# Six elementwise operations of the back stages issued on GpSimd instead of VectorE, with the beats planned anew

## The reference

```python
x = x + layernorm(attn(layernorm(x)))     # a selective state space layer ("front" and "back")
x = x + layernorm(ffn(layernorm(x)))      # mixture of low-rank experts ("back" and "last")

def attn(x, ...):                          # di = 512, N = 16 states
    h = x * rsqrt(mean(x * x) + EPS) * norm_scale
    xs, res = split(h @ w_in, 2)
    res, xs = silu(res), silu(causal_depthwise_conv(xs) + b)
    delta, B, C = split(xs @ w_xproj, ...)
    delta = softplus(delta @ w_dt + b_dt)
    ys = scan over the 512 tokens of (exp(delta * A), delta * xs * B), per channel and state
    out = (sum over the states of ys * C + xs * D) * res
    return x + out @ w_out

def ffn(x, ...):                           # two branches of 8 experts of rank 64
    prod = (x @ V_k) * cumsum(x @ W_k over tokens)
    weights = softmax(gelu(x @ r1 + b1) @ r2 + b2 + expert_bias)
    out = sum over k of (prod * weights) @ U_k + weights @ b
    return out / n_valid                   # n_valid = 1 .. number of the token
```

## Time and profile before

| | us |
|---|---|
| median of 3 runs | 2735.68 |
| lowest and highest run | 2731.32, 2737.05 |
| the profiled execution: first to last instruction | 2733.1 |
| VectorE busy in it | 2470.7 (90%) |
| TensorE busy (matmuls) | 2233.0 (82%) |
| ScalarE busy | 1718.4 (63%) |
| GpSimd busy | 1638.1 (60%) |

### The profile page before, as it was taken

How to read it: one execution, slowest core, us unless ns; L and a number is a source line. 1 busy time by engine, 2 the same in 40 slices (tenths; PEclk the granted TensorE clock), 3 DMA queues, 4 the chain that set the end, 5 groups by cost and what they waited for, 6 DMA issues and landing times.

```text
span 2733.1 us, 35478 instructions
## 1 busy us (share of the span) xinstructions
PE 2233.0 (82%) x9268; PEld 1316.2 (48%) x9268; DVE 2470.7 (90%) x3315; ACT 1718.4 (63%) x3353; POOL 1638.1 (60%) x1083
## 2 busy tenths in 40 slices
PE   5666788888888888888888888888888888888798
PEld 2434355454544545454454545445454554545454
DVE  1699999999999999999999999999999999999951
ACT  3554675858567584766758476675847667584544
POOL 0667575757657575665757566575756757575610
PEclk9766899999999999999899998999999999999998
DMA  5011100101001010110101010010101001010100
GB/s 123 24 43 31 42 25 28 51 28 51 29 20 55 28 52 24 51 32 21 56 26 53 24 51 29 24 55 24 55 25 51 28 24 55 24 47 28 35 1 16
DMA packets 83410, 101.81 MB, mean 37 GB/s; under 512 B 23481, under 2 KB 49873, under 8 KB 83169
## 3 DMA queue, kind: packets, MB, share of 16 engines
q1 hardware_dynamic: 83168, 99.06, 12.2%
HBM read 90.13 MB, written 8.91 MB: 36 GB/s over the span
## 4 chain that ended last, share of the span: by engine, by line
DVE 37%; issue 27%; PE 14%; POOL 11%; ACT 5%; DVEq 1%; POOLq 0%; ACTq 0%
DVE h L1252 13%; DVE yT L1268 11%; PE bank L709 9%; POOL bx L680 7%; PE stateT L878 3%; DVE xs L1127 3%; DVE prod L1227 2%; ACT decay L1084 2%; ACT cum_sb L1049 2%; DVE res L1148 1%; DVE yT L1265 1%; POOL x_back L646 1%; DVE xs L1142 1%; PE bank L853 1%; DVE st L1107 1%
## 5 line engine op out<-in xcount | busy, mean ns | idle before, releaser
L680 POOL TENSOR_TENSOR bx<-dx,B_rows 128x1024 f32<-128x1024 f32 x512 | 1219.5, 2389 | 495.6 <-DVE h L1252 468.7
L1252 DVE TENSOR_TENSOR_SCAN h<-decay,bx 128x512 f32<-128x512 f32 x1024 | 1238.3, 1209 | 75.8 <-ACT decay L1084 52.0
L1084 ACT ACTIVATE decay<-delta,decay_rate 128x512 f32<-128x512 f32 x1024 | 706.8, 693 | 656.6 <-DVE h L1252 631.6
L878 PE MATMUL stateT<-ident,h 128*128 128x128 f32 x4096 | 683.6, 298 | 322.0 <-DVE h L1252 175.8
L878 PEld LDWEIGHTS stateT<-ident,h 128*128 128x128 f32 x4096 | 499.0, 150 | 725.5 <-issue 353.4
L1268 DVE SCALAR_TENSOR_TENSOR yT<-stateT,C_tok,yT 128x512 f32<-128x512 f32 x960 | 696.0, 725 | 16.3 <-PE stateT L878 16.0
L709 PE MATMUL bank<-q_to_expert,xnT 128*128 128x512 f32 x512 | 267.3, 649 | 12.5 <-ACT dx L988 12.4
L709 PE MATMUL bank<-k_to_expert,cumT 128*128 128x512 f32 x512 | 266.7, 647 | 9.3 <-DVE prod L1227 9.2
L709 PE MATMUL bank<-hT,w_in_sb 128*128 128x512 f32 x512 | 245.7, 610 | 18.1 <-DVE xs L1127 17.2
L1049 ACT ACTIVATE cum_sb<-bank,gate 128x64 f32<-128x64 f32 x1024 | 222.8, 329 | 39.4 <-PE bank L709 28.3
L853 PE MATMUL bank<-expert_to_out,prodT 128*128 128x256 f32 x1024 | 242.1, 379 | 0.4 <-ACT prodT L1059 0.4
(11 more groups left out here) (161 smaller groups left out, 2493.1 us busy)
## 6 DMA issues: line engine op xcount, KB each, us to landing
B_rows<-B_scratch SPq DMA_DIRECT2D x256, 256.0 KB, 3.2
x_front<-in_L_attn_x SPq DMA_DIRECT2D x16, 512.0 KB, 4.5
x_back<-in_L_attn_x SPq DMA_DIRECT2D x16, 512.0 KB, 5.1
out<-x_back SPq DMA_DIRECT2D x16, 512.0 KB, 3.3
w_in_sb<-in_L_attn_w_in SPq DMA_DIRECT2D x1, 1024.0 KB, 5.7
h<-in_L_ffn_V_fwd SPq DMA_DIRECT2D x2, 256.0 KB
h<-in_L_ffn_W_inv_exp SPq DMA_DIRECT2D x2, 256.0 KB
h<-in_L_ffn_W_fwd SPq DMA_DIRECT2D x2, 256.0 KB
```

The source lines that it names most:

```text
L680: pool.tensor_tensor(bx[use % BX_RING][:, :, :], dx[q.parity][:, 2 * half:2 * half + 2, :], row, ALU.mult).then_inc(s_bx.step(f"{n},{half} ...
L878: last = pe.transpose(stateT[j % 2][:, c * P:(c + 1) * P], h[n % 2][:, c, j * P:(j + 1) * P], ident[:, :])
L1084: act.activation(decay[c % 2][:, :], delta[q.parity][:, c, :], ACT.Exp, scale=decay_rate[:, c, n:n + 1]).then_inc(s_exp.step(f"{n},{c}"), 1)
L1252: dve.tensor_tensor_scan(h[n % 2][:, c, :], decay[c % 2][:, :], bx[(2 * n + c // 2) % BX_RING][:, c % 2, :], 0.0, ALU.mult, ALU.add).then_ ...
```

## The change

The six operations keep, o, x1, sub, sn and wa go from VectorE's list to GpSimd's, with their semaphore steps (b_dve to b_pool), and everyone who waits for them waits for the other semaphore. keep becomes a tensor_scalar multiplication by 1. n_valid is replaced by its reciprocal once in VectorE's prologue, so that rc takes the reciprocal of sm's result at once and sn multiplies after it; before, sn came first. In TIMETABLE many beats are new.

```diff
-    ("B", "keep", "dve"): (255,),
+    ("B", "keep", "pool"): (264,),
-    ("F", "rs", "pool"): (15,),
+    ("F", "rs", "pool"): (18,),
-    ("F", "x", "sp"): (86,),
+    ("F", "x", "sp"): (79,),
...
-    ("F", "dt", "act"): (89, 93, 107, 111),
-    ("F", "ex", "act"): (91, 94, 107, 119),
-    ("F", "ln", "act"): (92, 96, 107, 119),
+    ("F", "dt", "act"): (89, 90, 107, 114),
+    ("F", "ex", "act"): (91, 95, 107, 119),
+    ("F", "ln", "act"): (92, 96, 109, 119),
...
-    ("F", "row", "sp"): (102, 123, 126),
+    ("F", "row", "sp"): (99, 123, 126),
-    ("B", "u", "dve"): (263, 264, 264, 268),
-    ("B", "o", "dve"): (268, 270, 271, 271),
-    ("B", "wo", "pe"): (274, 278, 282, 287),
-    ("B", "r", "dve"): (283, 283, 287, 289),
-    ("B", "st", "dve"): (293,),
+    ("B", "u", "dve"): (263, 264, 264, 270),
+    ("B", "o", "pool"): (273, 275, 278, 278),
+    ("B", "wo", "pe"): (274, 280, 282, 287),
+    ("B", "r", "dve"): (283, 286, 287, 289),
+    ("B", "st", "dve"): (290,),
...
-    ("B", "t", "act"): (302,),
-    ("B", "x1", "dve"): (301,),
+    ("B", "t", "act"): (301,),
+    ("B", "x1", "pool"): (304,),
...
-    ("B", "rb1", "pool"): (309,),
-    ("B", "xn", "act"): (310,),
+    ("B", "rb1", "pool"): (317,),
+    ("B", "xn", "act"): (315,),
...
-    ("B", "gelu", "act"): (338,),
+    ("B", "gelu", "act"): (337,),
...
-    ("B", "lb", "dve"): (346,),
-    ("B", "mx", "dve"): (347,),
-    ("B", "sub", "dve"): (347,),
-    ("B", "ex", "act"): (348,),
-    ("B", "sm", "dve"): (349,),
-    ("B", "sn", "dve"): (351,),
-    ("B", "rc", "dve"): (352,),
-    ("B", "wa", "dve"): (353,),
+    ("B", "lb", "dve"): (345,),
+    ("B", "mx", "dve"): (346,),
+    ("B", "sub", "pool"): (354,),
+    ("B", "ex", "act"): (347,),
+    ("B", "sm", "dve"): (347,),
+    ("B", "sn", "pool"): (359,),
+    ("B", "rc", "dve"): (349,),
+    ("B", "wa", "pool"): (359,),
...
-    ("L", "t", "act"): (468,),
+    ("L", "t", "act"): (469,),
-    ("F", "dx", "pool"): (105, 113, 126, 127),
+    ("F", "dx", "pool"): (103, 111, 126, 127),
...
+            def keep_task(b, k, use):
+                if b.shift(-1).exists:
+                    pool.wait_ge(b_dve.sem, b_dve.done(b.shift(-1), "r3"))
+                pool.wait_ge(f_pool.sem, f_pool.done(b, "r1"))
+                pool.sem_inc(passed["pool"], 1)
+                pool.tensor_scalar(r_keep[:, :], r_x0[b.parity][:, :], 1.0, None, ALU.mult).then_inc(b_pool.step("keep"), 1)
+
+            def o_task(b, c, use):
+                r = b.parity
+                pool.wait_ge(b_dve.sem, b_dve.done(b, f"u{c}"))
+                pool.tensor_tensor(res[r][:, c, :], xs[r][:, c, :], res[r][:, c, :], ALU.mult).then_inc(b_pool.step(f"o{c}"), 1)
...
+            def sub_task(b, k, use):
+                pool.wait_ge(b_dve.sem, b_dve.done(b, "mx"))
...
             def wo_task(b, k, use):
                 if k == 0:
-                    pe.wait_ge(b_dve.sem, b_dve.done(b, "o3"))
+                    pe.wait_ge(b_pool.sem, b_pool.done(b, "o3"))
...
             def soft_exp(b, k, use):
-                act.wait_ge(b_dve.sem, b_dve.done(b, "sub"))
+                act.wait_ge(b_pool.sem, b_pool.done(b, "sub"))
...
                 dve.wait_ge(w_pool, 7)
+                dve.reciprocal(n_valid[:, :, :], n_valid[:, :, :]).then_inc(w_dve, 1)
```

More of the change, by code:

```diff
@@ L320, in program @@
         b_act = Steps(sem("b_act"), steps_of("act", "B", {"t": numbered("t"), "xn": numbered("xn"), "xnT": ["xnT{}"], "rt": ["rt{}"], "gelu": ["gelu"], "logit": ["lc"], "ex": ["ex"], "gT": ["gT"]}))
[L321 to L325, removed]
+        b_dve = Steps(sem("b_dve"), steps_of("dve", "B", {"u": ["u{}"], "r": ["r{}"], "st": numbered("st"),
+                                                          "ag": numbered("ag"), "st1": numbered("s1"), "ag1": numbered("a1"),
+                                                          "cum": ["cum{}"], "lb": ["lb"], "mx": ["mx"], "sm": ["sm"], "rc": ["rc"]}))
+        b_pool = Steps(sem("b_pool"), steps_of("pool", "B", {"keep": ["keep"], "o": ["o{}"], "rb": ["ve", "rb", "ng", "nm"], "x1": ["x1"],
+                                                             "rb1": ["ve1", "rb1", "ng1", "nm1"], "sub": ["sub"], "sn": ["sn"], "wa": ["wa"]}))
         l_pe = Steps(sem("l_pe"), steps_of("pe", "L", {"cum": ["cum{}"], "xv": ["xv{}"], "pt": ["pt{}"], "out": ["out{}"]}))
@@ L646, in x_task, with x1_task, sn_task, wa_task @@
                 pool.tensor_tensor(x_back[b.parity][:, half, :], x_back[b.parity][:, half, :], o_rows[:, half, :], ALU.add).then_inc(l_pool.step(f"x{k}"), 1)
+            def keep_task(b, k, use):
[8 more added lines that the diff above has]
+                pool.tensor_tensor(res[r][:, c, :], xs[r][:, c, :], res[r][:, c, :], ALU.mult).then_inc(b_pool.step(f"o{c}"), 1)
+            def x1_task(b, k, use):
+                pool.wait_ge(b_act.sem, b_act.done(b, "t3"))
+                pool.tensor_tensor(x_back[b.parity][:, :, :], x_back[b.parity][:, :, :], rows[:, :, :], ALU.add).then_inc(b_pool.step("x1"), 1)
+            flat_l = logits[:, :, :, :].rearrange("p a b k -> p (a b) k")
+            def sub_task(b, k, use):
+                pool.wait_ge(b_dve.sem, b_dve.done(b, "mx"))
+                pool.tensor_tensor(flat_l, flat_l, top[:, :].rearrange("p (a o) -> p a o", o=1).broadcast_to([P, TB * 2, KE]),
+                                   ALU.subtract).then_inc(b_pool.step("sub"), 1)
+            def sn_task(b, k, use):
+                pool.wait_ge(b_dve.sem, b_dve.done(b, "rc"))
+                pool.tensor_tensor(total[:, :], total[:, :], n_valid[:, :, :].rearrange("p a b -> p (a b)"), ALU.mult).then_inc(b_pool.step("sn"), 1)
+            def wa_task(b, k, use):
+                pool.wait_ge(b_pool.sem, b_pool.done(b, "sn"))
+                if b.shift(-1).exists:
+                    pool.wait_ge(l_act.sem, l_act.done(b.shift(-1), "cum7"))
+                pool.tensor_tensor(gate[:, :, :].rearrange("p a (b k) -> p (a b) k", k=KE), flat_l,
+                                   total[:, :].rearrange("p (a o) -> p a o", o=1).broadcast_to([P, TB * 2, KE]), ALU.mult).then_inc(b_pool.step("wa"), 1)
             def back_rstd(b, k, use):
@@ L810, in gateT_task @@
             def gateT_task(b, k, use):
-                pe.wait_ge(b_dve.sem, b_dve.done(b, "wa"))
+                pe.wait_ge(b_pool.sem, b_pool.done(b, "wa"))
                 if use.sem is b_dve.sem:
@@ L941, in xs_task @@
                     if b.shift(-2).exists:
-                        act.wait_ge(b_dve.sem, b_dve.done(b.shift(-2), "o3"))
+                        act.wait_ge(b_pool.sem, b_pool.done(b.shift(-2), "o3"))
                 act.wait_ge(f_pe.sem, f_pe.done(b, f"xs{c}"))
@@ L1046, in cum_task @@
                         act.wait_ge(l_dve.sem, l_dve.done(b.shift(-1), "pr7"))
-                    act.wait_ge(b_dve.sem, b_dve.done(b, "wa"))
+                    act.wait_ge(b_pool.sem, b_pool.done(b, "wa"))
                 for k in range(KE):
@@ L1153, in r_task @@
                     dve.wait_ge(xb_in[b.parity], b.half_count(16, 16))
-                    dve.wait_ge(b_dve.sem, b_dve.done(b, "keep"))
+                    dve.wait_ge(b_pool.sem, b_pool.done(b, "keep"))
                     if b.shift(-1).exists:
@@ L1167, in ag_task @@
                 aggregate(b_dve, b, st_b, mv_b, "st", "ag")
-            def x1_task(b, k, use):
-                dve.wait_ge(b_act.sem, b_act.done(b, "t3"))
-                dve.tensor_tensor(x_back[b.parity][:, :, :], x_back[b.parity][:, :, :], rows[:, :, :], ALU.add).then_inc(b_dve.step("x1"), 1)
             def st1_task(b, k, use):
-                dve.wait_ge(b_dve.sem, b_dve.done(b, "x1"))
+                dve.wait_ge(b_pool.sem, b_pool.done(b, "x1"))
                 stats(b_dve, x_back[b.parity], st_1, "s1")
@@ L1205, in sm_task, with rc_task @@
                 dve.tensor_reduce(total[:, :], flat_l, AX.X, ALU.add).then_inc(b_dve.step("sm"), 1)
-            def sn_task(b, k, use):
+            def rc_task(b, k, use):
                 dve.wait_ge(b_dve.sem, b_dve.done(b, "sm"))
-                dve.tensor_tensor(total[:, :], total[:, :], n_valid[:, :, :].rearrange("p a b -> p (a b)"), ALU.mult).then_inc(b_dve.step("sn"), 1)
-            def rc_task(b, k, use):
-                dve.wait_ge(b_dve.sem, b_dve.done(b, "sn"))
                 dve.reciprocal(total[:, :], total[:, :]).then_inc(b_dve.step("rc"), 1)
[L1215 to L1220, removed]
             def pr_task(b, u, use):
```

63 lines of the change are left out of this document (27 added, 36 removed).

## The result

The changed kernel takes 2573.64 us (median of four runs, 2569.22 to 2579.97), against 2735.01 for the kernel before on the same chip: a ratio of 0.9415, 95% interval 0.9399 to 0.9431. 161 us are gone; the forecast was 2598, a gain of 138. The profiled spans say the same, 2733.1 to 2572.9, so 160.2 us less.

What follows compares the result with a forecast made beforehand. VectorE was taken as the bound (2470.7 of 2733.1 us busy). Removable 11.0 us a period, less 1.0 and 0.7, gives 9.3; times 15, 139.5 off 2735.7, plus 1.5 for the tail: 2598 us, range 2565 to 2655.

Steps and rivals of the forecast that it cites:

- the inner waits: VectorE operations with two SBUF operands wait for the GpSimd operation in progress; removable with the moves: 11.0 us a period.
- It fits with almost nothing over: Early slots: wo0, waiting for o3, ends at 14.2 us; VectorE wants the state transposes behind it at 14.7.
- wo0's wait on GpSimd's res about 1 to 2 us: Sign to look for: TensorE's wo0 waits about 1 to 2 us for o's result from GpSimd.
- the longer wait for decay near the softmax: Sign to look for: VectorE idle for decay near the softmax about as long as before plus 1.
- Case 5: Slower through wo0: o3 12.8 us late becomes VectorE's stall; +3.5 us a period, 2790 us, chance 0.03.
- I charge 0.5 there: First four slots: 0.5 us a period of the gain lost to TensorE, in order and coupled to every scan.
- The 93%: First four slots: TensorE's share, 31.17 us of work in about 33.3 left after o's 4.9 and keep's 1.2.
- At that rate 26.15 takes 27.8: Softmax stretch: ScalarE's 26.15 us at its densest 94% takes 27.8 of 30.1, so 2.3 us is gained.
- the 3.7: Softmax stretch: removable us a period from moving sub, sn and wa; 2.7 of it expected to be collected.
- The tail was charged 1.5: Tail after the last scan: 1.5 us added, x1 at 2.39 instead of 1.23 plus small handovers.
- the 0.4 of L t and the 1.7 of t that pay for x1: Beat changes: L t behind a decay gives back 0.4 us; t before a decay about 1.7, against x1's extra 1.2.
- The fourth case: Slower: only free 4.6 us leave VectorE, 8.6 exposed on GpSimd; +4.0 us a period, 2796 us, chance 0.02.

Runs made afterwards that it cites:

- d_two: The changed kernel with 64 small two-SBUF-operand multiplications of 128x8 added on VectorE, output unused: 2697.95 us, 0.9855 of the kernel before.
- u_o: The changed kernel with o alone back on VectorE (u3 and o at their old beats): 2694.49 us, 0.9863 of the kernel before.
- u_soft: The changed kernel with only sub, sn and wa back on VectorE: 2621.12 us, 0.9584 of the kernel before.
- u_keep: The changed kernel with keep alone back on VectorE: 2605.05 us, 0.9524 of the kernel before.
- d_cp: The changed kernel with 64 SBUF-to-SBUF copies of 128x8, one operand, added on VectorE, output unused: 2695.86 us, 0.9858 of the kernel before.
- rs15: The changed kernel with the front's rstd chain alone back at beat 15 on GpSimd, ahead of a bx and o0: 2641.91 us, 0.9659 of the kernel before.
- m_old: The six moves to GpSimd, with every beat of unmoved tasks as in the kernel before (rc at 350): 2693.53 us, 0.9860 of the kernel before.
- warm: The changed kernel with the state transposes of slot 9, beat 6 issued four times over, same result: 2550.54 us, 0.9324 of the kernel before.
- u_all: The changed kernel with all six operations back on VectorE, the other new beats kept except those that follow them: 2744.74 us, 1.0034 of the kernel before.

## Why the prediction was right, and where it was off

**Right: bound, mechanism and prices.** VectorE busy was forecast near 2290 and is 2291.9; o on GpSimd 1.272 us and 1.274 measured; sub and wa 0.33 and 0.30; keep and sn 0.20, and 0.24 and 0.21 measured; x1 2.39 and 2.36. GpSimd's busy time came to 1752 where 1775 was forecast. I can't put all of that apart; 13 us of it are the 512 bx, whose mean fell from 2389 to 2363 ns: before, 43 of them took over 2.5 us, after none. That the inner waits vanish rather than move was argued from one timeline; d_two shows them directly, and u_o, u_soft and u_keep give them back. The rule was stated too narrowly, for two SBUF operands: keep is a copy with one, and d_cp shows that those wait too. The sum was unharmed, since keep's price came from its own row.

**Right: wo0, within 0.4 us.** The chain of events around o was forecast within 0.4 us at each step. "It fits with almost nothing over" was the correct reading: rs15 brings o3 3.6 us later and loses 68 us, m_old more. Of my signs, "wo0's wait on GpSimd's res about 1 to 2 us" was wrong, it waits 0.26 before its weight load, and so was the longer wait for decay near the softmax (below). Case 5 had the right place, a wrong order on GpSimd, but also said that a delay is VectorE's stall one for one; rs15 shows that only where the clock stays up (o3 3.6 us late, VectorE idle for 3.2 in slot 2). In the other periods it is dearer, 4.6 to 5.4, since TensorE's idle gap is followed there by the lower clock; in m_old its next matmuls take 3.78 us instead of 1.99.

**Off: the charges, by 1.0 us a period, and what was left out.** The forecast was 9.3 a period and 139.5 in the stretch of scans, where 158.5 were measured.
- "I charge 0.5 there", TensorE in the first slots: slots 1 to 3 gave 5.01, all of o's 4.9. The charge was nothing. The 93% was not reached either: it took keep's 1.2 us out of slots 0 to 3, but keep stood in slot 15, so 34.3 us were left and TensorE worked 30.16 of them, 88%. That in order was no loss: VectorE has no idle time there.
- "At that rate 26.15 takes 27.8", the softmax: 2.49 collected and 2.7 forecast, so the size was right, but by luck. The mechanism was not: I had charged a wait for decay, and that wait fell by 1.0 us a period; what ate the gain were stateT, 1.1, and w2, 0.95. The new beats carry 2 us of ScalarE's work out of the stretch (24.16 in 26.7, 90%), and a period with slot 10 at the full clock gives 3.4 of the 3.7 (26.7 against 30.1). The mean is lower for TensorE's clock in slot 10, a cost that I had not priced at all; warm removes it.
- d1 was named only as a danger. In fact its mean fell from 874 to 773 ns, 6.4 us in all, about 0.4 a period (slots 13 and 14): before, 16 of the 64 started while a bx ran, after none.
- Slots 15 and 0 gave 1.56 and 1.2 was forecast: VectorE's idle time at the loop's edge went from 2.3 to 1.7 a period.
- The stretch of scans has more than my 15 equal periods of back work: batch 0's keep (2.1 us in the first period) and the last, 8.5.
- The tail was charged 1.5 and got 1.1 shorter. x1 is dearer there as forecast (2.36 for 1.23), yet the running sum behind it starts 42.9 us behind the last scan, 43.3 before, and the logits 61.2 against 62.3. I did not follow which of the beats did this.

In sum 19.0 us in the scans, 2.6 in the tail and 0.6 in the front: the 22 us by which the span beat the forecast.

**Half seen: what the beats are for.** The prediction went through the beats as a service to the moves and credited them with the 0.4 of L t and the 1.7 of t that pay for x1. m_old says that 120 of 161 us hang on them, u_all that without the moves they are worth nothing. The two are not a sum but one design: the moves free the time, the order on GpSimd and TensorE decides whether it can be had.

**The engine rule.** The fourth case, the Trainium skill's Engine selection in GPSIMD Engine Reference taken literally, would have been 2796 us. Its ratio of two holds (1274 against 657 ns), and its advice fails here: it prices the instruction and not the wait inside it. 114 us of work on GpSimd replace 179 us on VectorE.

**What stays open.** x1 was not put back alone; with all six back, slot 5, where it stands, is 1.3 us longer a period. The parts put back one at a time (121, 47.5, 31.4 us) add up to more, 200, than all six together, 171. Slot 10 is counted in each: it is 0.6, 0.5 and 0.6 us longer a period in the three, and 0.2 in u_all. How much of the rest of each part is clock was not separated. Why the clock falls behind the gap in nine periods of twelve and not in the other three, with the same gap in all, is not shown.

## What to carry to other kernels

Where two engines meet inside an instruction, take each small operation's minimum and median duration in place: 157 against 1898 ns says that the operation costs its neighbour's duration, and moving it to the slower engine can pay. Moving alone gave 41 us here, and the order around the moved work 120 more, so look first at what the receiving engine does ahead of the result that the next engine waits for. Look then at short idle gaps of TensorE ahead of long matmuls: a few repeated transposes bought 23 us, most of it in the slot behind the gap.

## What had not been expected of the hardware

- A copy with one SBUF operand waits for a running GpSimd instruction like an operation with two (1901 and 1898 ns in the median, each ending 20 to 34 ns behind it), a reduction with one does not (205 to 217 ns).
- An idle gap of 1.9 us of TensorE was followed in some periods by the clock at its lower level and in others not: the same eight matmuls 3.61 and up to 5.95 us. Twelve more 128x128 transposes in the gap ended that for these matmuls in every period looked at; the clock fell later instead, where it cost nothing.
- That loss reaches VectorE only where it has nothing else to do: the same edit gained 23 us in the changed kernel and about 3 in the one before, where slot 10 takes 10.09 us at either clock.
